# An adaLN layer with linear attention and eight experts: row statistics and centring one block further ahead, and a new order of projections, score strips and activations

## The reference, in short

```python
mod = (silu(c) @ wmod).reshape(16, 6, 1, 256)        # shifts, scales, gates of each of 16 rows
sa, ca, ga, sb, cb, gb = ...                         # |ga|, |gb| kept at 0.25 or above
h = layernorm(x) * (1 + ca) + sa                     # x: 16 x 512 x 256
q, k, v = phi(h @ W_q), phi(h @ W_k), h @ W_v        # heads of 64, phi = elu + 1
S_t = S_{t-1} + k_t v_t^T;  z_t = z_{t-1} + k_t      # causal linear attention
o_t = (S_t q_t) / max(z_t . q_t, 1e-6)
x = x + ga * (o @ W_o)
h = layernorm(x) * (1 + cb) + sb
# router: top 2 of 8 experts by softmax of layernorm(h) @ router_w
# expert e: gelu(layernorm_e(h) @ w1[e] + b1[e]) @ w2[e] + b2[e], weighted and summed
x = x + gb * experts(h)
```

## Time and profile before

| | us |
|---|---|
| median of 3 runs | 1125.62 (1122.92 to 1125.95) |
| the profiled execution's own time | 1125.48 |
| its span | 1123.6 |
| TensorE busy | 988.9 (88%) |
| VectorE busy | 889.1 (79%) |
| ScalarE busy | 542.9 (48%) |
| GpSimd busy | 573.6 (51%) |

### The profile page before, as it was taken

One profiled execution on the slowest core, in us unless ns is written; L12 is line 12 of the kernel. 1 busy time (PEld: TensorE's weight loads), 2 busy tenths in 40 slices (PEclk: granted clock), 3 DMA queues, 4 the chain that ended last, 5 costly groups with the idle time before them and its releaser, 6 DMA issues.

```text
span 1123.6 us, 31567 instructions
## 1 busy us (share of the span) xinstructions
PE 988.9 (88%) x8116; PEld 806.3 (72%) x8117; DVE 889.1 (79%) x3010; ACT 542.9 (48%) x1123; POOL 573.6 (51%) x478
## 2 busy tenths in 40 slices
PE   5777879887945099999999999999999999999997
PEld 1334545554534088888888888888888888888875
DVE  5578999999985567777877877877877877877776
ACT  1668787878843134434444443444443443444443
POOL 2121666666667536655455445445445445545543
PEclk8798888888965599999999999999999999999999
DMA  4465777876869466665565555566555556566453
GB/s 134 133 227 194 237 230 260 291 271 212 315 233 401 122 185 132 137 123 92 96 118 98 106 112 104 98 109 99 94 108 103 90 108 108 87 120 122 88 100 49
DMA packets 162626, 169.80 MB, mean 151 GB/s; under 512 B 89340, under 2 KB 136968, under 8 KB 158472
## 3 DMA queue, kind: packets, MB, share of 16 engines
q1 hardware_dynamic: 129736, 114.24, 36.5%
q0 software_dynamic: 32832, 54.88, 25.3%
HBM read 94.67 MB, written 62.78 MB: 140 GB/s over the span
## 4 chain that ended last, share of the span: by engine, by line
PE 66%; issue 8%; DVE 8%; POOL 6%; ACT 2%; DMA 1%; POOLq 0%; DVEq 0%; SPq 0%; ACTq 0%
PE banks L1440 32%; PE banks L1452 31%; POOL lists L551 5%; PE banks L1334 2%; DVE st L771 2%; POOL rs L544 2%; DVE store L968 1%; PE banks L1322 1%; ACT rowbuf L628 1%; DVE mv L779 1%; ACT store L712 1%; DVE rowbuf L908 1%; DMA out<-rowbuf,ydst 0%; DVE store L926 0%; DVE ix L1001 0%
## 5 line engine op out<-in xcount | busy, mean ns | idle before, releaser
L1440 PE MATMUL banks<-nhl,store 128*128 128x256 bf16 (+1 forms) x3408 | 450.5, 268 | 28.0 <-DMA nhl<-xhl 24.8
L740 ACT ACTIVATE gf<-banks,b1t 128x256 f32<-128x256 f32 (+1 forms) x568 | 263.0, 463 | 429.1 <-PE banks L1440 411.7
L1452 PE MATMUL banks<-store 128*128 x3240 | 448.0, 273 | 0.5
L1440 PEld LDWEIGHTS banks<-nhl,store 128*128 x3408 | 324.1, 98 | 71.0 <-issue 30.1
L587 POOL DMA_INDIRECT out<-rowbuf,ydst x135 | 223.7, 1657 | 294.1 <-DVE rowbuf L1222 222.0
L1452 PEld LDWEIGHTS banks<-store 128*128 128x128 bf16 x3240 | 310.5, 98 | 41.9 <-issue 1.8
L1231 DVE CAST store<-gf 128x256 bf16<-128x256 f32 (+1 forms) x568 | 180.5, 318 | 130.7 <-ACT gf L740 99.3
L1233 DVE TENSOR_TENSOR store<-gf,store 128x256 bf16<-128x256 f32 (+1 forms) x568 | 234.7, 413 | 19.5
L551 POOL DMA_INDIRECT lists<-store,slot x128 | 141.0, 1102 | 96.3 <-issue 49.0
L578 POOL DMA_INDIRECT store<-y_rows,ygb x135 | 135.2, 1001 | 63.3 <-issue 51.8
L544 POOL TENSOR_TENSOR rs<-ve,mhalf 128x12 f32<-128x12 f32 (+2 forms) x20 | 39.0, 1950 | 84.6 <-DVE ve L786 84.5
(11 more groups left out here) (225 smaller groups left out, 970.0 us busy)
## 6 DMA issues: line engine op xcount, KB each, us to landing
rowbuf<-lists SPq DMA_DIRECT2D x64, 264.0 KB
store<-in_L_ffn_w SPq DMA_DIRECT2D x16, 1024.0 KB, 6.0
wsplit<-store SPq DMA_DIRECT2D x16, 1024.0 KB, 5.7
store<-wsplit SPq DMA_DIRECT2D x16, 1024.0 KB, 11.1
b2t<-in_L_ffn_b SPq DMA_DIRECT2D x71, 128.0 KB
store<-in_L_attn_x SPq DMA_DIRECT2D x16, 512.0 KB, 9.6
out<-store SPq DMA_DIRECT2D x16, 512.0 KB, 9.9
csB<-mod_rows SPq DMA_DIRECT2D x16, 256.0 KB, 4.0
```

What stands on the lines that cost most here:

```text
L740: a.activation(gf[:, c % 2, 0:halves(j) * P], MM[c % 2][:, 0:halves(j) * P], ACT.Gelu, bias=b1t[:, r, c:c + 1]).then_inc(gf_s, 1)
L1440: last = t.matmul(MM[c % 2][:, 0:halves(j) * P], w, nhl[:, r, m, 0:halves(j) * P], start=n == 0, stop=n == 5)
L1452: last = t.matmul(ACC[r][h][:, 0:D], g[:, c, h * P:(h + 1) * P], w, start=c == 0 and n == 0, stop=c == NI - 1 and n == 2)
```

## The change

The change has four parts. No arithmetic is added or removed, apart from a narrower slice at the border steps.

1. **Statistics one block further ahead.** VectorE takes `stats` and `moments` of x for block i+2 in step i (was i+1), so one more set of statistics, one more `inverse_root` and one more `neg_mean_rstd` stand before step 0. The x loads go one block further ahead with them: blocks 2 and 3 before step 0, block i+3 in step i. VectorE's `neg_mean_rstd` moves behind the split of the weights (L940, L946).
2. **Centring one block further ahead.** ScalarE centres block i+1 in step i, after the copies of `oz`, instead of block i at the head of step i (`centred`). ScalarE no longer waits for `nm` at the head of a step but behind `hT`, which moves forward to stand right behind `ktok` and the b1 copy.
3. **TensorE's projections are split.** q and k go in front of the scores, with a semaphore of their own (`projq_s`). v stays behind the rank sums (`proj_s`).
4. **Relu and Exp go in front of the strip copies** on ScalarE. The copy of v goes behind the routing's normalisation.

Besides, the router's bias sum on VectorE moves from the set-up into step 0, and TensorE's wait for it into step 1. The core of the diff, in which "..." marks what is left out:

```diff
-            return slice(0 if i < NB else 1 if i - 3 < NB else 2, 1 if i < 3 else 2 if i < 4 else 3)
+            return slice(0 if i + 1 < NB else 1 if i - 3 < NB else 2, 1 if i < 3 else 2 if i < 4 else 3)
...
+            def load_block(b):
+
+                sp.wait_ge(got_x[b % 2], 16 * (b // 2))
+                sp.dma_start(resid[:, b * NC:(b + 1) * NC, :], x_v[b]).then_inc(got_x[b % 2], 16)
...
+            for b in range(2, 4):
+                load_block(b)
             sp.wait_ge(mod_step, 8)
...
+                if 0 < i < NB - 3:
+                    load_block(i + 3)
...
+            def centred(b, r):
+
+                act.wait_ge(got_x[b % 2], 16 * (b // 2) + 16)
+                wait_past(act, xT_s, b)
+                normalise(lambda c: xc[:, c, :], rows(b), r, 0, xc_s)
+
+            act.wait_ge(nm_s, 1)
+            centred(0, 1)
+
             def step(i, half, r, project, attend, settle, norm, route, place):
-                if project or norm or route:
-                    act.wait_ge(nm_s, i + 1)
-                if project:
-                    act.wait_ge(got_x[r], 16 * half + 16)
-                    wait_past(act, xT_s, i)
-                    normalise(lambda c: xc[:, c, :], rows(i), r, 0, xc_s)
...
+                if project:
+
+                    act.wait_ge(xT_s, i + 1)
+                    act.wait_ge(modc_s, i + 1)
...
+                    last.then_inc(hT_s, 1)
+                if i + 1 < NB or norm or route:
+                    act.wait_ge(nm_s, i + 2)
...
                 if project:
-
-                    act.wait_ge(xT_s, i + 1)
-                    act.wait_ge(modc_s, i + 1)
...
+                    act.wait_ge(projq_s, i + 1)
+                    wait_past(act, phi_s, i)
+                    a.activation(ex[:, :], Q[:, :], ACT.Relu, scale=-1.0).then_inc(exn_s, 1)
+                    act.wait_ge(exn_s, i + 1)
+                    a.activation(ex[:, :], ex[:, :], ACT.Exp, scale=-1.0).then_inc(ex_s, 1)
+                if i == 0:
+                    centred(1, 0)
                 if attend:
                     b = i - 1
                     act.wait_ge(score_s, b + 1)
...
+                if 0 < i < NB - 1:
+                    centred(i + 1, r)
...
-            var_eps(0, 1)
+            var_eps(-1, 1)
+            dve.wait_ge(got_x[1], 16)
+            stats(rows(1), 0)
+            neg_mean_rstd(-1, 1)
+            moments(0, 1)
+            var_eps(0, 2)
...
-                    stats(rows(i + 1), 0)
+                    stats(rows(i + 2), 0)
...
-                if project or attend or norm:
-                    neg_mean_rstd(i + 1, 1 - r)
+                if i == 0:
+                    router_bias()
                 if project and r == 1:
...
+                if project or attend or norm:
+                    neg_mean_rstd(i + 1, 1 - r)
...
+                if project:
+                    pe.wait_ge(hT_s, i + 1)
+                    if r == 0:
+                        wait_past(pe, phi_s, i)
+                    else:
+                        pe.wait_ge(b1r_s, half + 1)
+                    for k in range(NK):
+                        last = t.matmul(Q[:, :], wqk[:, k, :], hT[:, k, :], start=k == 0, stop=k == NK - 1)
+                    last.then_inc(projq_s, 1)
                 if attend:
                     b, q = i - 1, 1 - r
```

More of the change, by code:

```diff
@@ L646, in step @@
                     a.activation(b1rows, Q[0:H + 1, :], ACT.Copy).then_inc(b1r_s, 1)
+                if project:
+                    act.wait_ge(xT_s, i + 1)
+                    act.wait_ge(modc_s, i + 1)
+                    wait_past(act, proj_s, i)
+                    hold(act, "act")
+                    for k in range(NK):
+                        last = a.activation(hT[:, k, :], TR[k][:, :], ACT.Identity,
+                                            bias=modc[:, r, 2 + k:3 + k], scale=modc[:, r, k:k + 1])
+                    last.then_inc(hT_s, 1)
+                if i + 1 < NB or norm or route:
+                    act.wait_ge(nm_s, i + 2)
                 if norm:
@@ L657, in step @@
                 if project:
-                    act.wait_ge(xT_s, i + 1)
-                    act.wait_ge(modc_s, i + 1)
-                    wait_past(act, proj_s, i)
-                    hold(act, "act")
-                    for k in range(NK):
-                        last = a.activation(hT[:, k, :], TR[k][:, :], ACT.Identity,
-                                            bias=modc[:, r, 2 + k:3 + k], scale=modc[:, r, k:k + 1])
-                    last.then_inc(hT_s, 1)
+                    act.wait_ge(projq_s, i + 1)
[5 more added lines that the diff above has]
+                    centred(1, 0)
                 if attend:
@@ L821, in _ @@
             moments(0, 0)
-            var_eps(0, 1)
+            var_eps(-1, 1)
+            dve.wait_ge(got_x[1], 16)
+            dve.wait_ge(mv_s, 1)
+            hold(dve, "dve")
+            stats(rows(1), 0)
+            neg_mean_rstd(-1, 1)
+            dve.wait_ge(nm_s, 1)
+            dve.wait_ge(ve_s, 1)
+            moments(0, 1)
+            var_eps(0, 2)
             dve.wait_ge(mod_ps, 1)
@@ L886, in step @@
                     v.tensor_tensor(diag, diag, causal[:, :].unsqueeze(1).to_broadcast([P, NC, P]), ALU.mult).then_inc(diag_s, 1)
-                if project and not (isinstance(i, int) and i == NB - 1):
-                    if r == 0:
-                        dve.wait_ge(got_x[1], 16 * half + 16)
-                    else:
-                        dve.wait_ge(got_x[0], 16 * half + 32)
+                if i + 2 < NB:
+                    dve.wait_ge(got_x[r], 16 * half + 32)
                     hold(dve, "dve")
-                    stats(rows(i + 1), 0)
+                    stats(rows(i + 2), 0)
                 if norm:
@@ L905, in step @@
                 if norm:
-                    b, q = i - 3, 1 - r
                     dve.wait_ge(h2m_s, b + 1)
@@ L1347, in step @@
                 if project:
-                    pe.wait_ge(hT_s, i + 1)
-                    if r == 0:
-                        wait_past(pe, phi_s, i)
-                    else:
-                        pe.wait_ge(b1r_s, half + 1)
                     wait_past(pe, ktok_s, i)
-                    for k in range(NK):
-                        t.matmul(Q[:, :], wqk[:, k, :], hT[:, k, :], start=k == 0, stop=k == NK - 1)
                     for k in range(NK):
```

43 lines of the change are left out of this document (17 added, 26 removed).

## The result

| | before | after |
|---|---|---|
| median (us) | 1124.41 (4 runs, 1122.92 to 1125.95) | 1135.27 (4 runs, 1130.5 to 1143.79) |
| ratio | | 1.0105, 95% interval 1.0074 to 1.0136 |
| span of the profiled execution (us) | 1123.6 | 1136.3 |

The changed kernel is 1% slower. The forecast was 1118.5 us, faster; the time lies 7 us above the upper end of its range, 1128 us. Times and ratios are those of fast executions; e5, e6 and e13 had one slow execution each, left out, and the profile of e6 is of its slow one.

A forecast was written before the change was run, and what follows sets the result against it. VectorE's own chain, 18.8 us a step, was taken to bound the first phase's middle; the second phase stays untouched. Statistics -1.7, `nm` -3.0, start -1.3, middle -1.0 sum to -7.0: 1125.5 to 1118.5 us, range 1110 to 1128.

The forecast's parts named there:

- the odd step of the middle: Steps 4 to 14, b1 product ahead of transposes: ranks ready 0.6 us early at full clock, 2.4 us late at half.
- A second one comes in front of the router's transposes: TensorE's second idle gap per step, where q and k used to fill in; named without a size of its own.
- the sum had -1.0: Term for steps 4 to 14: two steps at half-clock price, +3.4 us, the rest without rank waits, -4.4 us.
- Removed statistics, -1.7: VectorE, steps 4 to 14: ten sets of statistics instead of eleven, 1.41 us plus an estimated 0.3 us saved.
- `nm` behind the split, -3.0: End of the first phase: waits of 0.93 and 2.29 us hidden under the split; almost no loss in the middle.
- The start, -1.3: Steps 1 to 3: -0.9 us from step 1's mask, expected between 40.7 and 46.3 us, and -0.4 in steps 2 and 3.
- The 0.33 us ahead of phi (L926): ScalarE in the middle: a wait now and then, expected to go because phi finds `ex` ready.
- The slower one: Rival: bound moves to TensorE's chain from phi to ranks, +18 us in the middle, +14 overall, 1140 us; chance 0.13.
- the mark set for it: Sign of the slower rival: VectorE's rank-sum waits exceed 8 us in all, or ScalarE's strips hold the mask.
- Right marks missed: Signs if right, end of phase: `nm` waits under 1 us in step 16, gap before step 17's scatters under 1 us.
- The rule that spoke against: TensorE's clock: taken strictly, it opposed putting the bigger burst, q and k, behind a gap; linked to the slower rival.

The follow-up runs named there:

- e5: The changed kernel with part 4 alone undone (Relu, copy of v and Exp behind the router's normalisation again): ratio 1.0119 to the kernel before.
- e6: The changed kernel with `nm` in front of the split of the weights again: ratio 1.0122 to the kernel before.
- e13: The changed kernel with parts 3 and 4 undone and three unread matmuls between transposes of x and score strips, a repeat run: ratio 0.9907 to the kernel before.
- second pair: Profiles of the kernel before and the changed kernel, both unchanged, together on another chip: ratios 0.9999 and 1.0144 to the kernel before.
- e16: The same kernel as e13, one execution for its profile beside e15 on one chip: first expert matmul 12.9 us sooner than e15.
- e7: The changed kernel with parts 3 and 4 undone, statistics and centring still one block ahead, a repeat run: ratio 0.9967 to the kernel before.
- e12: The changed kernel with parts 3 and 4 undone and `nm` in front of the split again: ratio 0.9994 to the kernel before.
- e11: The kernel before with only `nm` moved behind the split of the weights: ratio 1.0181, 1169.83 against 1149.17 us.
- The fillers: Extra 128x512 matmuls with unread results in TensorE's gaps; two before the router's transposes in the changed kernel gave 0.9963, again 0.9951, of the kernel before.
- e4: The changed kernel with the router's normalisation and the second layernorm's centring exchanged on ScalarE: ratio 0.9998 to the kernel before.
- c_after: The changed kernel, unchanged, run again for profile and time on another chip: ratio 1.0144 to the kernel before.
- e15: The kernel before, unchanged, one execution for its profile beside e16 on one chip; no ratio given.
- c_before: The kernel before, unchanged, as a control with a profile on the chip of c_after: ratio 0.9999.

## Why the prediction was wrong, point by point

- **The step that failed** is the odd step of the middle: "TensorE's own part, b1 product 1.88 and transposes 1.0, is done by 3.5", counted from phi's end, and with it "counted from phi's end" as the head of the chain. I took W_o as finished by then, without a row for it. In the first long step the b1 product began 6.0 us behind phi's end (143.58 and 137.62) and the transposes ended at 9.4. The chain starts at the strips, not at phi.
- **The gap that was seen and not priced.** "A second one comes in front of the router's transposes, where q and k used to fill in" is the cause, 2.17 us in nearly every step. I priced half clock on q, k and scores, where it cost little (19.9 us a step), and put it at nothing on the logits and W_o, where it cost 2.8 to 5.4 us in three steps and 0.7 in a fourth. From the mask of step 4 (92.33 and 92.91, 0.6 ahead) to that of step 15 (315.35 and 301.70, 13.7 behind) the kernel lost 14.2 us; for that stretch the sum had -1.0 and, for the statistics, -1.7. (In the second pair the same stretch lost 15.2 us.)
- **Removed statistics, -1.7:** the size was right where no other loop held VectorE (1.4 us in e16). In the changed kernel it was under the loss.
- **`nm` behind the split, -3.0:** 1.0 us in step 15, as forecast. In step 16 `nm` still waited 2.71 us, because of the stretched scatter, and the stretch behind it gave 0.1 us (2.7 in the second pair, inside the spread). "In the middle ... they lose next to nothing" held (e7 against e12), but only thanks to part 2; e11 shows the edit alone at +20.7 us.
- **The start, -1.3:** -2.3 at step 1, inside the bounds given (40.7 to 46.3; 42.14 came), and -0.6 by step 4 (92.33 instead of 92.91). That is no confirmation: in the second pair it was -0.5 at step 1 (42.74 and 43.27) and +2.3 at step 4 (92.94 and 90.67). The kernel before alone differs by 2.2 us at step 4 between its two profiles, so the term is neither shown nor refuted.
- **A misread row.** The 0.33 us ahead of phi (L926) was counted as a wait for `ex`; the row says "issue", no wait that the profile shows, and it stands unchanged in the new order, where `ex` is ready (L945, 136.93 us).
- **The rivals.** The slower one (1140 us, 0.13) had the sign and nearly the time, and the mark set for it, rank waits over 8 us, was met with 14.4. But its chain is not the one at work: it puts the price on q, k and the scores at half clock. Right marks missed: `nm` in step 16 waits 2.71 us, and the gap before step 17's scatters is 2.36 us (3.59 before), not under 1.
- **The rule that spoke against.** The Trainium skill, "TensorE: Matmul & The Clock Gate", section "HAM oscillation — how this bites in real kernels", says that matmul bursts parted by waits are paid for at the low clock, in each burst. The trace agrees in part: behind the same gap of 2.17 us W_o ran at half clock in four steps and at full clock in the others. The fillers agree from the other side: 0.82 granted with the gap, 0.96 without. I had applied it to one gap and weighed it at two steps of eleven.

## What to carry to other kernels

When an instruction is moved, ask what it leaves behind as well as what it stands ahead of: price the hole in the engine that it used to cover, with every matmul behind the hole that lies on the step's loop at its half-clock duration. In a pipeline over in-order engines, count the whole loop of a step round to its own start, and from the latest predecessor, not from the event that is easiest to find. And where TensorE waits in each step, a few matmuls whose result nobody reads are a cheap test, and here a gain, since they cost nothing as long as they end before the wait does.

## What the runs showed of the hardware

- **GpSimd's instructions took longer beside VectorE's split of the weights.** In step 16 the scatter beside it took 3.03 or 3.04 us instead of 0.96 in every profile but one with `nm` behind the split. In that one, e4, it was the power, 3.71 us instead of 1.67. Even before, the scatter that began half way through the split took twice its time. In each case GpSimd was done 0.8 to 1.5 us after VectorE's instruction ended. e4, VectorE and GpSimd:

```profile
328.05 2.29 DVE L965 TENSOR_TENSOR store<-store 128x2048 bf16<-128x2048 f32 x1
```

```profile
328.17 3.71 POOL L546 TENSOR_TENSOR rs<-ve,mhalf 128x8 f32<-128x8 f32 x1 [0.38 <-issue]
```

and the kernel before, GpSimd beside the split of 328.82 us:

```profile
330.03 1.92 POOL L551 DMA_INDIRECT lists<-store,slot  x1 [0.30 <-issue]
```

- **The same gap does not always cost the clock.** 2.17 us of idle in each step led to half clock all through W_o in four steps, the same four in two executions (after and c_after), and in three steps in e5. What picks them out is open.
- **Chips differ.** The kernel before had medians of 1124 to 1125 us in the runs of the result and on chip 3, and of 1149 to 1154 on chips 0, 5, 11 and 15. Up to step 16 its masks agree within 3.2 us, and the difference lies behind: in e15 81.0 us instead of 74.0 (76.3 in c_before) from there to the first expert matmul, and 756 instead of 729 us in the second phase.
